# Edge attention in a graph kernel: key rows added by the gather onto edge features, the one-hot on VectorE, tile numbers read at the head of each window

## The reference, cut to what matters

```
q, k, v = (xn @ Wq + bq), (xn @ Wk + bk), (xn @ Wv + bv)       # per node, 8 heads of 32
ep      = ef @ We + be                                         # per edge, 32, shared by the heads
scores  = einsum('ehd,ehd->eh', q[dst], k[src] + ep[:, None, :]) * scale * ew[:, None]
m       = segment_max(scores, dst);  ex = exp(scores - m[dst])
attn    = ex / segment_sum(ex, dst)[dst]
out     = segment_sum(attn[:, :, None] * v[src], dst)          # then @ Wo + bo
```

## Time and profile before

| | |
|---|---|
| median of three runs | 4696.7 us (4696.5 to 4701.38) |
| the profiled execution | 4699.27 us |
| its span, first to last instruction | 4697.5 us |
| mean granted TensorE clock | 0.811 of full |
| PE busy | 3211.3 us (68%) |
| DVE busy | 2496.5 us (53%) |
| POOL busy | 1926.7 us (41%) |
| ACT busy | 1568.2 us (33%) |
| DMA packets, mean over the span | 112 GB/s |

### The profile page before, as it was taken

The page is one execution under the profiler, slowest core; times in us unless marked ns, Lnnn a source line. Parts: engine busy times, 40 slices in busy tenths (PEclk is TensorE's granted clock), DMA queues, the critical chain, the costliest instruction groups (busy, mean ns, idle before and its releaser), DMA issues. The chain is left out here.

```text
span 4697.5 us, 64474 instructions
## 1 busy us (share of the span) xinstructions
PE 3211.3 (68%) x12643; PEld 2346.8 (50%) x12644; DVE 2496.5 (53%) x5566; ACT 1568.2 (33%) x3419; POOL 1926.7 (41%) x1857
## 2 busy tenths in 40 slices
PE   1577777777673991674477777777777777449594
PEld 1466566556341781342255555555555555336463
DVE  4443333333251004347587877877777777761314
ACT  0333333333320230141244444444444444222221
POOL 1777777777104004000545445454545454220001
PEclk9677777777785995786688888988888898669797
DMA  3755555555101662300555555554555555200000
GB/s 92 203 145 145 144 144 143 141 144 139 29 1 56 199 210 79 121 13 12 155 136 148 142 138 150 139 146 132 151 139 140 149 142 145 97 23 0 18 0 30
DMA packets 339646, 525.74 MB, mean 112 GB/s; under 512 B 169022, under 2 KB 229962, under 8 KB 335696
## 3 DMA queue, kind: packets, MB, share of 16 engines
q0 software_dynamic: 114432, 353.45, 27.3%
q1 hardware_dynamic: 224892, 170.78, 13.3%
q10 hardware_dynamic: 260, 0.80, 0.0%
HBM read 462.21 MB, written 63.83 MB: 112 GB/s over the span
## 5 line engine op out<-in xcount | busy, mean ns | idle before, releaser
L2187 POOL DMA_INDIRECT store<-kv_d,flash_index x832 | 869.8, 1045 | 888.3 <-PE flash_sums L2231 644.4
L717 POOL DMA_INDIRECT agg_rows<-xn_d,agg_index x832 | 795.1, 956 | 320.7 <-issue 224.2
L810 PE MATMUL agg_sums<-agg_rows,agg_member 128*128 128x257 f32 x1664 | 577.3, 508 | 230.2 <-ACT agg_rows L730 130.5
L2220 PE MATMUL flash_query<-q,flash_mem_t 128*128 x1664 | 501.2, 453 | 239.3 <-DVE store L2392 93.6
L810 PEld LDWEIGHTS agg_sums<-agg_rows,agg_member 128*128 128x128 f32 x1664 | 403.4, 257 | 384.8 <-ACT agg_rows L730 272.2
L730 ACT ACTIVATE agg_rows<-agg_rows,weight_of 128x256 f32<-128x256 f32 x832 | 369.9, 500 | 640.7 <-DMA agg_rows<-xn_d,agg_index 638.3
L2231 PE MATMUL flash_sums<-store,flash_member 128*128 128x264 f32 x1664 | 460.3, 423 | 174.8 <-DVE acc L2465 144.5
L2220 PEld LDWEIGHTS flash_query<-q,flash_mem_t 128*128 128x128 f32 x1664 | 344.8, 225 | 336.2 <-issue 281.5
L786 DVE TENSOR_TENSOR acc<-acc,agg_sums 128x257 f32 x416 | 176.5, 424 | 589.5 <-PE agg_sums L810 539.8
L2231 PEld LDWEIGHTS flash_sums<-store,flash_member 128*128 128x128 f32 x1664 | 322.3, 205 | 296.1 <-DVE acc L2465 131.3
L2305 ACT ACTIVATE flash_mem_t<-flash_wide,minus_row 128x512 f32<-128x512 f32 x208 | 142.9, 687 | 574.2 <-PE flash_wide L2209 574.2
(11 more groups left out here) (398 smaller groups left out, 4698.4 us busy)
## 6 DMA issues: line engine op xcount, KB each, us to landing
expert_w<-in_L_ffn_W_dram SPq DMA_DIRECT2D x64, 512.0 KB, 4.5
agg_feats<-in_ef_t_dram SPq DMA_DIRECT2D x52, 512.0 KB, 6.9
agg_rows<-xn_d,agg_index POOLq DMA_INDIRECT x832, 2.8
ep_d<-agg_ep SPq DMA_DIRECT2D x52, 256.0 KB
store<-kv_d,flash_index POOLq DMA_INDIRECT x832, 3.8
flash_ep<-ep_d SPq DMA_DIRECT2D x416, 32.0 KB
flash_flags<-flags_d SPq DMA_DIRECT2D x416, 32.0 KB
xs_d<-zeros SPq DMA_DIRECT2D x1, 8448.0 KB, 30.9
```

The lines of the kernel that those rows point to most:

```text
L717: pool.indirect_dma_start(rows[:, q, 0:D], None, sh.xn_d, bass.IndirectOffsetOnAxis(ap=index[:, q:q + 1], axis=0)).then_inc(gathered[u], 16)
L810: last = pe.matmul(sums[:, u % 4, 0:W], member[:, u % WI * SUBS + k, :], rows[:, q, :], start=(k == 0), stop=(k == SUBS - 1))
L2187: pool.indirect_dma_start(ring[:, s, :], None, sh.kv_d, bass.IndirectOffsetOnAxis(ap=index[:, s:s + 1], axis=0)).then_inc(gathered[p][g], 16)
L2220: last = pe.matmul(query[:, c * D:(c + 1) * D], mem_t[:, g % 2, c * P:(c + 1) * P], sh.q[:, bass.ds(t, 1), :], start=True, stop=True)
```

## The change

1. `add` is gone from DVE. The gather's indirect DMA adds (`compute_op=ALU.add`) onto what the slot holds. For that ACT fills each slot first (`prepare`): zeros under the values and the edge features, repeated for the eight heads, under the keys. A new semaphore `slot_ready` counts the filled groups; POOL waits for it instead of `sums_done`, and SP waits for it instead of `mult_done` before it overwrites `ep`. The wait for the edge features moves from DVE to ACT, the wait for the gather moves into `mult`.
2. `belong` goes from ACT to DVE, as one comparison of 128x512 for each group.
3. The tile numbers of a body are read in one list at its head, eight `value_load`s; `rescale` and `keep` use them.

```diff
@@ SP, load
-                        sp.wait_ge(mult_done, G * w - G)
+                        sp.wait_ge(slot_ready, G * w - G)
@@ POOL, gather
-                        hold(pool, sums_done, WI * w + (2 * g + 2), pool_ticks)
+                        hold(pool, slot_ready, G * w + (g + 1), pool_ticks)
...
-                                                    bass.IndirectOffsetOnAxis(ap=index[:, s:s + 1], axis=0)
-                                                    ).then_inc(gathered[p][g], 16)
+                                                    bass.IndirectOffsetOnAxis(ap=index[:, s:s + 1], axis=0),
+                                                    compute_op=ALU.add).then_inc(gathered[p][g], 16)
@@ ACT
-                def belong(a, g):
...
+                def prepare(s, g):
+                    hold(act, sums_done, WI * s.at + (2 * g + 2), act_ticks)
+                    if g == 0:
+                        act.wait_ge(ep_in[s.side], 16 * WI * s.turn)
+                    r = ring[:, s.side * WS + 4 * g:s.side * WS + 4 * g + 4, :]
+                    act.activation(r[:, :, HI_].rearrange("p k (h v) -> p k h v", h=H),
+                                   sh.zeros[:, 0:VW].unsqueeze(1).unsqueeze(1).to_broadcast([P, 4, H, VW]), ACT.Copy)
+                    act.activation(r[:, :, LO].rearrange("p k (h d) -> p k h d", h=H),
+                                   ep[:, s.side, 4 * g:4 * g + 4, :].unsqueeze(2).to_broadcast([P, 4, H, DH]), ACT.Copy)
+                    act.drain().then_inc(slot_ready, 1)
+
+                for g in range(G):
+                    prepare(Window(0, 0, 1), g)
+                for g in range(G - 1):
+                    prepare(Window(1, 1, 1), g)
@@ ACT, body: belong 0 to 3 gone; prepare(s, 3) after place(s, 1); prepare(after(s), 0 to 2) at the end
...
@@ DVE
-                def add(s, g):
...
+                def belong(a, g):
+                    dve.wait_ge(sums_done, WI * a.at + (2 * g + 2 * WI - 2))
+                    dve.tensor_tensor(member[:, g % 2, :, :], sh.lane[:, :].unsqueeze(1).to_broadcast([P, 4, P]),
+                                      sh.lane_of[:, bass.ds(WS * a.at + 4 * g, 4)].unsqueeze(2).to_broadcast([P, 4, P]),
+                                      ALU.is_equal).then_inc(member_ready, 1)
@@ DVE, mult
                     dve.drain()
+                    dve.wait_ge(gathered[s.side][g], 64 * s.turn)
                     dve.wait_ge(query_ready, G * s.at + (g + 1))
@@ DVE, body
+                    if a is not None:
+                        tiles = [dve.value_load(sh.tile_id[0:1, bass.ds(WI * a.at + n, 1)], min_val=0, max_val=NT - 1)
+                                 for n in range(WI)]
...
```

More of the change, by code:

```diff
@@ L2115, in stage_flash @@
         sums_done = sem("sums_done")
+        slot_ready = sem("slot_ready")
         added = sem("added")
@@ L2322, in body @@
                         place(s, 0)
-                    else:
-                        belong(a, 0)
                     if s is not None:
                         place(s, 1)
-                    if a is not None:
-                        belong(a, 1)
-                    if s is not None:
+                        if a is not None:
+                            prepare(s, 3)
                         place(s, 2)
@@ L2346, in body @@
                         place(after(s), 0)
-                    if a is not None:
-                        belong(a, 2)
-                        belong(a, 3)
+                        if a is not None:
+                            for g in range(G - 1):
+                                prepare(after(s), g)
                 windows(act, body)
@@ L2445, in lower, with rescale @@
                     dve.tensor_tensor(low[:, :], st, top[:, :], ALU.subtract).then_inc(p_ready, 1)
-                def rescale(a):
-                    t = dve.value_load(sh.tile_id[0:1, bass.ds(WI * a.at, 1)], min_val=0, max_val=NT - 1)
+                def rescale(a, tiles):
+                    t = tiles[0]
                     dve.drain()
@@ L2457, in weigh, with keep @@
                     dve.tensor_tensor(r, r, e.unsqueeze(3).to_broadcast([P, 4, H, VW]), ALU.mult).then_inc(pv_ready, 1)
-                def keep(a, g):
+                def keep(a, g, tiles):
                     for n in range(2):
-                        t = dve.value_load(sh.tile_id[0:1, bass.ds(WI * a.at + (2 * g + n), 1)], min_val=0, max_val=NT - 1)
+                        t = tiles[2 * g + n]
                         dve.drain()
@@ L2470, in body @@
                                         ).then_inc(index_ready, 1)
-                    if s is not None:
-                        add(s, 0)
                     if a is not None:
@@ L2480, in body @@
                     if s is not None:
-                        add(s, 1)
                         mult(s, 1)
@@ L2486, in body @@
                     if s is not None:
-                        add(s, 2)
                         mult(s, 2)
@@ L2490, in body @@
                     if a is not None:
-                        rescale(a)
+                        rescale(a, tiles)
+                        belong(a, 0)
                         weigh(a, 0)
-                    if s is not None:
-                        add(s, 3)
-                    if a is not None:
+                        belong(a, 1)
                         weigh(a, 1)
-                        keep(a, 0)
+                        keep(a, 0, tiles)
                     if s is not None:
@@ L2502, in body @@
                     if a is not None:
+                        belong(a, 2)
                         weigh(a, 2)
-                        keep(a, 1)
+                        keep(a, 1, tiles)
+                        belong(a, 3)
                         weigh(a, 3)
-                        keep(a, 2)
+                        keep(a, 2, tiles)
                     if ffn is not None and ffn[1] == 1:
@@ L2512, in body @@
                     if a is not None:
-                        keep(a, 3)
+                        keep(a, 3, tiles)
                 windows(dve, body)
```

6 lines of the change are left out of this document (1 added, 5 removed).

## The result

The changed kernel takes 5132.74 us (four runs, 5125.46 to 5140.25), the kernel before 4698.56 us beside it (four runs). The ratio is 1.0924, with a 95% interval of 1.0901 to 1.0947: 434 us slower. The forecast was 4950 us, +4.7 us for a body of the stage; its range of 4775 to 5250 holds the time, its own narrower range (4780 to 5025) doesn't. The profiled execution took 5125.64 us with a span of 5123.9.

A forecast was written before the change was run, and what follows sets the result against it. No engine was full; DVE's fixed order, with PE answers between, bound the body. Terms summed to +3.7 us at full clock, +4.7 with the clock; 52 bodies (+244) and +8 gave 4950 us, range 4775 to 5250, narrower 4780 to 5025.

The forecast's parts named there:

- The main term: Head of a body on DVE: eight value loads in order, nearly unhidden, add 5.6 us (ends 4.4 and 6.8).
- the nearest rival: Gather queues: the adding gather is slow and becomes the bound, 5190 us at 2.4 us a gather; chance 0.15.
- Rival 1: Head of a body: the eight loads overlap and share one latency, 1.3 us in all, about 4655 us; chance 0.12.
- the 0.72 us a load: DVE's sequencer: one load with register arithmetic and assertion, taken between 0.58 and 0.87 us.
- Loads that go: DVE's `rescale` and `keep`: loads leaving their old places, four of them exposed at second additions, save 1.0 us a body.
- adds 0 and 3: DVE's order: nothing else stood ready there, so both removed adds count, saving 2.28 us a body.
- adds 1 and 2: Between the mults on DVE: removing them saves 1.05 us, as a PE ladder is late next; 9.4 instead of 10.44.
- The clock: PE around `ask` 1: six in ten bodies at the lower level, giving 38.9 us a body, +4.7 over the mean.
- Gathers: nothing: Gather path: adding costs the body nothing, with 1.9 us of queue, 1.25 of POOL and landing after 3.8.
- the floor of 36 us: Gather limit on a body: 16 gathers at 1.9 us, 1.5 between sums and filled slot, 3.8 of landing.
- Rival 2: Gather queues: the adding gather becomes the bound, deciding from 2.1 us a gather; 5610 us at 2.9; chance 0.15.
- The start: Stage start: gather 0 waits for edge features and a filled slot, about +8 us once.

The follow-up runs named there:

- e4_plain: The changed kernel with a plain gather that overwrites the filled slots instead of adding; 5421.78 us, 0.9956 of the kernel before on chip B.
- e2b_early: The kernel before with only the list of eight loads at the head; 5660.98 us, 1.0449 of the kernel before on chip C.
- e10_late_plain: The changed kernel with loads where they stood before and a plain gather; 4729.13 us, 1.0061 of the kernel before on chip D.
- e7_spread: The kernel before with its eight loads spread, one behind each mult and each reduce; 5340.18 us, 0.9871 of the kernel before on chip C.
- e1b_late: The changed kernel with its loads where they stood before, adding gather kept; 5243.02 us, 0.9681 of the kernel before on chip C.
- e8_new_spread: The changed kernel with loads spread behind mult and reduce, window 1's slots filled after the first `place`; 4970.39 us, 1.0572 of the kernel before on chip D.
- e3_belong: The kernel before with only `belong` moved from ACT to DVE; 4846.96 us, 1.0312 of the kernel before on chip D.

## Why the prediction was right, and where its sizes were off

The sign and the place (DVE's order at the head of a body) were right, and `ask` 1 ran at the lower clock level as forecast. The main term was too small, and the nearest rival was nearer than it looked.

**The list.** The mechanism was right: strictly one load behind another, an idle time put down to "issue", PE idle beside it. Rival 1 (loads that overlap) is refuted by the 7.5 us of the index copy. The step that failed in size is the 0.72 us a load. It measured (7.5 + 0.2) / 8 = 0.96. For loads in a row the 0.72 was right, as the 0.70 to 0.72 us of e4_plain shows; what failed was to keep the load's own 307 ns beside adding gathers. It grew to a median of 523 and a mean of 534 ns, 8 x 0.23 = 1.8 us a body, which is nearly the whole difference to 5.6. It takes the adding gathers, not the list: with plain gathers the median stays at 300 to 307 ns in a list, late or spread (e4_plain, e2b_early, e10_late_plain, e7_spread), and with adding gathers in flight single loads are long too (430 ns in `rescale` in e1b_late, 420 to 524 for the first six in e8_new_spread). What in the adding gathers lengthens a load stays open. The Trainium skill ("DMA: Bandwidth & Descriptors", section "Latency and other measured facts") gives such a load a floor of about 600 ns. The load instruction alone took 307 ns; with its arithmetic and assertion it is 0.58 to 0.96 us, near or above that floor. The saving by unrolling that the section speaks of did not come, with eight loads in a list.

**Loads that go, adds 0 and 3, adds 1 and 2.** Forecast -1.0, -2.28 and -1.05 at full clock. With `prepare` in, the adds were measured at -2.8 net (e10_late_plain less e3_belong), where -3.3 was forecast. That PE's ladder would be late next behind adds 1 and 2 was right: 2.30 and 1.66 us of idle time at mult 1 and 2, for query rows. At full clock the ladder from mult 0 to mult 2 took 9.34 us (e10_late_plain) for the forecast 9.4. The late loads were not measured alone on a chip like A; the idle time ahead of `keep`'s additions, where they stood, fell from 3.9 to 3.2 us a body (`acc` rows of the waits between 2450 and 3950 us, waits for sums in it): 0.7, where 1.0 was forecast.

**`belong`.** The price was right at 684 ns for an interpolated 0.69. I had let overlap take it to 0.6 of DVE's order; it took 0.55 (2.2 over four, e3_belong), and the other 0.7 us of that run stand between mult 0 and mult 2, with `ask` 1 at the lower level. ACT's side was not measured alone, with 1.09 + 1.04 = 2.13 us a group for 2.4.

**The clock.** A stretch of idle PE ahead of `ask` 1 was there (6.9 and 2.25 us), and `ask` 1 ran at the lower level in the body shown. Over all 50 bodies it took over 3 us in each and 3.7 or more, the whole of it at the lower level, in 35; before, in 17 and 14. Six bodies in ten at that level would have made mult 0 to mult 2 11.5 us; the mean is 11.9. That the list is what brings the fall isn't shown: in e3_belong it came without a list.

**Where the 7.6 us stand.** DVE's body cut at the starts of the index copy and of the mults, means of the 50 bodies of each trace in us:

| kernel | copy to mult 0 | mult 0 to 2 | mult 2 to 3 | mult 3 to next copy | body |
|---|---|---|---|---|---|
| before | 2.86 | 11.61 | 8.73 | 10.98 | 34.19 |
| after | 1.81 | 11.91 | 8.53 | 19.53 | 41.78 |
| e3_belong | 2.87 | 12.31 | 9.75 | 12.15 | 37.07 |
| e10_late_plain | 1.95 | 9.34 | 9.44 | 13.50 | 34.24 |
| e8_new_spread | 2.46 | 14.88 | 9.68 | 11.97 | 38.98 |

Up to mult 3 the changed kernel is 0.95 us shorter than before, and 8.55 us longer between mult 3 and the next copy. The forecast's own terms for that last stretch are the list, two comparisons and three of the four exposed loads: 5.6 + 1.2 - 0.75 = 6.05. Of the 2.5 us over it, the list's longer loads are 1.9; the rest was not taken apart. The mults are another 0.4 over the forecast's 11.5. This is the 2.9 us between +4.7 and +7.6.

**Gathers: nothing.** Right for the changed kernel, where no wait of DVE names a gather, but by luck of a cover. The queue time of 1.9 us was right; POOL's 1.25 and the landing of 3.8 us, both left as they were, became 1.85 and 5.7. With these the floor of 36 us rises: 16 x 1.88 + 1.5 + 5.7 = 37.3, and 39.0 was measured (e8_new_spread). The forecast's sum of the floor also has the wrong ring: the body waits for twelve gathers up to mult 2 and for the way from mult 2 to the next filled slot, 11.9 us, not for sixteen gathers and 1.5 us. So the list and the adding gather lie beside each other: alone the adding costs 4.7 us a body, the list on top of it 2.8. Rival 2 was to decide from queue times of 2.1 us; it decides already at 1.88, once the list is out of the way. What the list would cost alone, with plain gathers, was not measured on a chip like A.

**The start.** Forecast +8 us, measured +35 (72.9 against 37.8). The terms that the forecast gives (2.4 + 5.0 + 3.8 less an add) come to 10, not 8. Of the 35, 27.8 us lie ahead of mult 0 of the first window, and 6.6 are the first list, which the forecast counts among its 52. ACT in the start of the changed kernel, then PE:

```profile
2305.12 1.09 ACT L2317 ACTIVATE store<-zeros 128x1056 f32<-128x1056 f32 x1 [9.67 <-DMA flash_ep<-ep_d]
2306.12 1.04 ACT L2319 ACTIVATE store<-flash_ep 128x1024 f32<-128x1024 f32 x1
...
2311.70 0.69 ACT L2306 ACTIVATE flash_mem_t<-flash_wide,minus_row 128x512 f32<-128x512 f32 x1
```

```profile
2314.44 3.76 PE L2221 MATMUL flash_query<-q,flash_mem_t 128*128 x8 [30.42 <-issue]
```

`prepare` for window 1 waits 9.67 us for the edge features of window 1, and the one-hot for the very first `ask` (L2306) is queued behind it on ACT. I had counted the filling that gather 0 waits for, and not what stands behind it on ACT. In e8_new_spread, which fills window 1 behind the first `place`, the first body is 19 us shorter (53.6); 6.6 of that is the list, which isn't there, so the order gave about 13.

## What to carry to other kernels

- An instruction of a sequencer cost nothing here behind a long instruction of its own engine. Gathered into a list at the head it was paid in full.
- Work moved from a busy engine into a DMA is paid in three places: queue time, issue time and landing. Follow all three round the ring of waits, from a buffer's release to its next one, and not only the one that grew most plainly. It can also lengthen small things beside it, here the register loads.
- Judge a time by its place. The 2.9 us of `belong` looked like four comparisons of 0.68 us with nothing hidden; cut at the mults, 0.7 of them stood where no `belong` is.
- When two parts of a change lie beside each other, taking one away shows little. Price each against the kernel in which the other is gone (34.24 here), or both look cheap.

## What the runs showed of the hardware that was not expected

**An adding gather of 128 rows of 2080 bytes** costs 1.55 us of POOL for 0.95, 1.88 us of the 16 queues for 0.96, and lands after 5.7 us for 3.8. The plain one, under the changed kernel's code (e10_late_plain):

```profile
L2188 POOL DMA_INDIRECT store<-kv_d,flash_index x832: 947/953/1812, 2279.9 to 4049.2; - x167
```

**A register load from SBUF is not of fixed length.** On DVE it went from 307 ns to a mean of 534 in the list at the head, with adding gathers in flight. With them in flight it was long outside a list too (420 to 524 ns in e8_new_spread, means by place), and with plain gathers its median stayed at 300 to 307 in every order tried.

**Chips differ by more than the change.** On chips B and C the kernel before takes 16 and 15% longer than on A and D. Some 255 us of it lie ahead of the stage, and within it the sequencers stand between single operations without a wait that the profile shows. SP's eight loads and DMAs of the edge features are the plainest row: the changed kernel (first) and e7_spread, both on chip C.

```profile
3325.30 8.54 SPq L2152 DMA_DIRECT2D flash_ep<-ep_d  x8
```

```profile
3310.80 20.18 SPq L2151 DMA_DIRECT2D flash_ep<-ep_d  x8
```

On chip A this row took 8.54 us. The changed kernel's stage is not lengthened on such a chip; that of e7_spread and e2b_early is, and by the total time (723 us, less 255, over 50) that of before by an estimated 9 us a body, of which there is no trace. Why the one program is spared and the others aren't stays open. The verdict on the change therefore hangs on the chip: 1.0924 on A, 0.9922 on C; for its parts I rely on A and D, where the kernel before takes the same time to 0.05%.
